# One graph kernel on Trainium2: the last 20 of 28 edge groups woven with the first 20 of 40 list groups

## The chip, the cores and the metric

The kernel runs on one core of a Trainium2 chip. The metric is device time in microseconds, the median of several executions. The core has TensorE (PE, matmuls and transposes), VectorE (DVE), ScalarE (ACT), GpSimd (POOL, which here issues all gathers and scatters) and SyncE (SP, which issues most plain DMAs). Each engine runs its own list of instructions in order and waits on semaphores for the others.

## The reference

Four graph layers over 100,000 nodes with 48 features and 50,000 edges, each followed by a residual sum and a layer norm. Cut to what matters:

```python
x = ln(x + gin(x))        # neigh = segment_sum(relu(x[src] + edge_feat), dst); (1 + eps) x + neigh
x = ln(x + appnp(x))      # 10 times: f = 0.9 * segment_sum(f[src] * w, dst) + 0.1 * x
x = ln(x + rgcn(x))       # relu MLP of 8 relations per edge, segment_sum over dst, relu
x = ln(x + edgeconv(x))   # segment_max over dst of theta(x[dst] - x[src]) + phi(x[src])
```

The kernel works on edges sorted by their target, in groups of 512 (`GE`). For edges whose source itself has incoming edges it keeps compact "lists", so that second-order terms (pairs), third-order terms and the later powers touch only list rows.

## The kernel before, in words

There are 100 edge groups (`NG`) and, for this input, 40 groups of the first list (the gather of the first pair stage is issued 160 times, four per group). `U = 4` groups make a turn. A chain of stages follows one another, each a `Block` on all five engines, closed by a barrier and by one semaphore clear after another on SP (`Scope.__exit__`, L102). The stages of interest:

- **Edge stage, tag `b_`** (`second_stage`, L1188 on; called with `FIRST = 7` turns, 28 groups). For each group, PE transposes the source rows (`columns`), applies the first weights for eight relations (`first`, three 128x512 matmuls in two passes), ScalarE applies relu (`hidden`), PE the second weights (`second`), DVE scales and scans along the edges (`weigh`, `add_up`, `highest`), PE turns the scans back into rows (`sums`), and DVE and ScalarE run three layer norms that trail by 0, 2 and 3 groups. The norm that trails by 3 groups ends in `norm4_end` (L1508, then the multiplication that writes `xob`, in the helper `scaled`, L1444). Four indirect DMAs on GpSimd (`scatter`, L1335, `after=3`) then write `xob` to the output. `part(work, i, s, k)` calls `work` for the group `k` back.
- The list of pairs is made ready meanwhile: `prepare_lines` and `run_lines` on DVE, `run_moves` on ScalarE after groups 0, 3, 4 and 7. Its last step (step 4, L1142) writes row 3 of `lists`.
- **First pair stage, `level(0, upper_rows)`**, tags `l_` in the profile (L1628 on). For each list group SP loads its numbers (`load`, L1668) and its keep row (`load_keep`), ScalarE casts the row numbers (`stage`), GpSimd gathers 4 x 128 rows of 97 floats (`fetch`, L281), DVE multiplies them by their weights (`message`, L1857 to L1864), PE transposes (`columns`), DVE scans (`add_up`, L1891), PE transposes back (`sums`), DVE takes row ends and compares places with column numbers (`run_end`, `one_hots`, L288), and PE packs the ends by 8 narrow matmuls (`pack_up`, L294), which SP stores (`put_list`).
- After it `prepare(1, ...)` and `level(1, ...)` follow, then `steps()`, where the other 72 edge groups (tag `e_`) run beside list groups of the powers, in an order written out by hand.

The order on GpSimd is what matters for the change. Before, the two stages have one kind of GpSimd work each:

```python
turns(pool, body, FIRST)      # edge stage: scatter of the group three back
drain(body, FIRST, 3)
...
part(fetch, i, s, 0, end)     # pair stage: the gather of each list group
```

Of the kernel before, what the change touches and what calls it, by code (L numbers as in the profile page):

```python
# [18 lines left out]
P, T = 128, 4  # L19
# [10 lines left out]
LINE = N // HP  # L30
EARLY = 32
FIRST = 7
WOVEN = 4
HALF = LINE // 2
ROWS = 20
# [75 lines left out]
def gnn(nc, a, out):  # L111
    ctx = ExitStack()
    with ctx:
# [89 lines left out]
        def slots(name, shape, dt=F32, n=U, scope=ctx):  # L203
            return [scope.enter_context(nc.sbuf_tensor(f"{name}{s}", shape, dt)) for s in range(n)]
# [920 lines left out]
        def run_moves(q, step):  # L1125

            (ends, firsts, places, carry), (s_places, s_chain, s_line, s_first, s_carry, s_out) = run_tiles, run_marks
            if step == 0:
                q.wait_ge(s_line, 1)
                q.dma_start(line_first[0].rearrange("(g e) -> g e", e=1), ends[1][:, 0:1]).then_inc(s_first, 16)  # L1130
            if step == 1:
                q.wait_ge(s_first, 16)
                q.dma_start(firsts[0][0:1, 0:NG], line_first[0].rearrange("(o g) -> o g", o=1)).then_inc(s_first, 16)
            if step == 2:
                q.wait_ge(s_line, 2)
                q.dma_start(line_first[1].rearrange("(o g) -> o g", o=1), firsts[1][0:1, 1:NG + 1]).then_inc(s_carry, 16)
# [13 lines left out]
        def prepare_lines(dve, k, made):  # L1150

            (now, before, after, keep, pen, kind), hot, (total, extra), (s_in, s_total, s_out, s_cnt, s_keep, s_end, s_hot) = made
            dve.wait_ge(s_total, 16)
            nc.vector.tensor_scalar(extra[:, :], total[:, :], float(GE * LU[k] - 1 - 3 * GE * LU[k]), float(GE * LU[k] * (WOVEN - 2)) if k == 2 else 0.0, ALU.add, ALU.max).then_inc(s_cnt, 1)
# [36 lines left out]
        def second_stage(scope, tag, lo, turns_n, psH, carried):  # L1191
# [18 lines left out]
            nb, kp = slots(f"{tag}nb", [F, GE], scope=scope), slots(f"{tag}kp", [XL, GE], scope=scope)  # L1210
# [62 lines left out]
            def scalar_part(act):  # L1273

                def square(k, i, s):
                    y, d, q = big[k]
                    d = rt[s][:, :, 2 * F:3 * F] if k == 2 else d
                    act.wait_ge(s_cen[k], i * U + s + 1)
                    nc.scalar.activation(q[:, :, :], d[:, :, :], ACT.Square).then_inc(s_sq[k], 1)
# [32 lines left out]
                def body(i, s, end=None):  # L1312
                    part(copy_x, i, s, 0, end)
                    part(lambda *z: square(2, *z), i, s, 0, end)
                    part(copy_d, i, s, 3, end)
# [225 lines left out]
        sc = slots("sc", [XL, GE], n=2)  # L1541

        with Scope(nc) as scope:
            first_list = preparation(0, scope)
            sync_part, scalar_part, pool_part, tensor_part, vector_part = second_stage(scope, "b_", 0, FIRST, bank[2:5], False)

            with nc.Block() as block:
                @block.sync
                def _(sp):
                    body, finish = sync_part(sp)  # L1550
                    turns(sp, body, FIRST)
                    drain(body, FIRST, 5)
                    finish()

                @block.scalar
                def _(act):
                    prepare_moves(act, 0, first_list, 3, 6)
                    run_moves(act, 0)
                    body = scalar_part(act)

                    def moving(i, s):
                        body(i, s)
                        if isinstance(i, int) and (i, s) in ((0, 0), (0, 3), (1, 0), (1, 3)):
                            run_moves(act, 1 + ((0, 0), (0, 3), (1, 0), (1, 3)).index((i, s)))

                    turns(act, moving, FIRST)
# [5 lines left out]
                def _(pool):  # L1572
                    run_places(pool)
                    body, finish = pool_part(pool, 3)
                    turns(pool, body, FIRST)
                    drain(body, FIRST, 3)
                    finish()

                @block.tensor
                def _(pe):  # L1580
                    head, tail = tensor_part(pe)

                    def body(i, s, end=None):
                        head(i, s, end)
                        tail(i, s, end)

                    turns(pe, body, FIRST)
                    drain(body, FIRST, 3)

                @block.vector  # L1590
                def _(dve):
                    parts = vector_part(dve)
                    dc = prepare_lines(dve, 0, first_list)

                    def body(i, s, end=None):
                        for work in parts:
                            work(i, s, end)
                        if isinstance(i, int) and (i, s) == (0, 2):
                            run_firsts(dve, dc)
                        if isinstance(i, int) and (i, s) == (1, 2):  # L1600
                            run_last(dve, dc)

                    turns(dve, body, FIRST)
                    drain(body, FIRST, 3)

        idxb, idx3, oi2, idxr = (sb(n, [P, NC], I32) for n in ("idxb", "idx3", "oi2", "idxr"))
        w_2 = sb("w_2", [P, NC])

        def first_rows(name, tables, clear):

# [287 lines left out]

                        drained(dve, body, 1, n)

        first_rows("pairs", level_rows[0:1], (idxb, idxr))
        level(0, upper_rows)
        prepare(1, 8, 10)
        level(1, level_rows[0])
        prepare(2, 12, 14)
# [867 lines left out]
```

## Time and profile before

| what | value |
|---|---|
| median of 3 runs | 4120.73 us (4113.66 to 4122.2) |
| the profiled execution | 4121.21 us, its span 4119.4 us |
| DVE, POOL, PE busy over the span | 69%, 63%, 60% |
| edge stage `b_`, from its first norm to its last scatter | 1358.9 to 1650.4 us |
| first pair stage, from its first load to its last store | 1669.2 to 1903.0 us |

Times in the trace count from the start of the span. A busy engine is not by itself the bound: the row to look for is the one that shows which wait of a stage ends last. The sum of the prediction is made against the profiled execution.

### The profile page before, as it was taken

The page shows a single profiled execution, that of the slowest core. Times are in us where ns is not written, and L with a number is a line of the kernel's source. Part 1 is how long each engine was busy: PE and PEld are TensorE (multiplying, and loading weights), DVE is VectorE, ACT ScalarE, POOL GpSimd, SP SyncE. Part 2 cuts the span into 40 slices and gives each one's busy share as a digit, 9 for nine tenths or more (in the row PEclk, how much of TensorE's full clock was granted, in tenths as well). Part 3 has the DMA queues.
Part 4 walks back from the last instruction along what each step waited for, and adds up shares of the span by engine and source line. Part 5 has one row for each costly group of instructions (what it writes and reads, how often), then busy time and mean ns, then how long its engine had stood idle before and what let it go on. Part 6 is the DMA issues. An engine that isn't in the chain of part 4 may idle for free. (4 is left out here: it accounts for less than half of the span.)

```text
span 4119.4 us, 57270 instructions
## 1 busy us (share of the span) xinstructions
PE 2456.7 (60%) x9282; PEld 1230.9 (30%) x9282; DVE 2823.3 (69%) x7287; ACT 1330.6 (32%) x4663; POOL 2604.9 (63%) x2529
## 2 busy tenths in 40 slices
PE   3730000277777797595644998888871009976664
PEld 2520000133333354231112554444440003333332
DVE  7989999799997787584322888887872325654333
ACT  0023333355554354131111444444431114431111
POOL 4747775377775144674754677767776766647776
PEclk9975555699999898797775999999985559985555
DMA  6947777688887443454225656656642662321111
GB/s 211 405 152 213 217 215 213 174 207 208 204 205 162 142 143 113 93 137 85 65 52 105 158 150 151 150 141 152 145 125 71 193 157 64 73 59 38 38 37 25
DMA packets 496345, 581.57 MB, mean 141 GB/s; under 512 B 218575, under 2 KB 369944, under 8 KB 491204
## 3 DMA queue, kind: packets, MB, share of 16 engines
q1 hardware_dynamic: 352858, 415.22, 32.9%
q0 software_dynamic: 87040, 90.63, 15.4%
q10 hardware_dynamic: 56306, 74.24, 5.7%
q14 instruction: 101, 0.83, 0.1%
q8 instruction: 40, 0.66, 0.1%
HBM read 276.73 MB, written 309.62 MB: 142 GB/s over the span
## 5 line engine op out<-in xcount | busy, mean ns | idle before, releaser
L505 POOL DMA_INDIRECT xdst<-in_x,dstc x400 | 459.0, 1147 | 233.5 <-issue 146.6
L281 POOL DMA_INDIRECT gb<-nodes,ib x400 | 386.7, 967 | 224.0 <-issue 126.2
L265 PE MATMUL bank<-ident,act 128*99 128x128 f32 x400 | 67.7, 294 | 645.3 <-ACT act L907 635.0
L1335 POOL DMA_INDIRECT out<-e_xob,e_ob x288 | 300.9, 1045 | 93.0 <-issue 85.6
L301 PE MATMUL bank<-chosen,rec 128*6 128x512 bf16 x1200 | 294.0, 398 | 0.6 <-ACT packed L898 0.6
L281 POOL DMA_INDIRECT cgb<-layer,ib x160 | 175.5, 1097 | 118.7 <-ACT ib L2403 72.2
L281 POOL DMA_INDIRECT ugb<-nodes,ib x160 | 166.4, 1040 | 128.8 <-ACT ib L1977 66.1
L265 PEld LDWEIGHTS bank<-ident,act 128*99 128x99 f32 x400 | 49.0, 171 | 658.0 <-issue 658.0
L294 PE MATMUL bank<-l_chosen,l_rec 128*3 128x512 f32 x480 | 242.3, 653 | 0.0
L1335 POOL DMA_INDIRECT out<-b_xob,b_ob x112 | 114.7, 1024 | 199.3 <-DVE b_xob L1444 173.4
L275 PE MATMUL bank<-ident,scan 99*128 99x99 f32 (+2 forms) x1120 | 199.5, 303 | 64.7 <-DVE scan L2170 34.1
L1384 PE MATMUL bank<-e_bxT,w 105*128 105x512 f32 x432 | 226.5, 640 | 9.3 <-ACT e_bxT L1290 8.7
L275 PEld LDWEIGHTS bank<-ident,scan 99*128 99x128 f32 (+2 forms) x1120 | 156.8, 212 | 242.7 <-issue 242.0
L1401 PE MATMUL bank<-mixer,sc 112*128 112x112 f32 x800 | 207.4, 403 | 28.1 <-issue 23.5
L1365 PE MATMUL bank<-e_hm,w 128*48 128x512 f32 x432 | 220.9, 651 | 0.0
L583 PE MATMUL bank<-hot_at,hot_no 128*125 128x400 f16 x800 | 156.0, 339 | 96.3 <-DVE hot_at L609 96.3
L281 POOL DMA_INDIRECT dgb<-layer,ib x160 | 156.2, 976 | 81.9 <-issue 47.8
L1401 PEld LDWEIGHTS bank<-mixer,sc 112*128 112x128 f32 x800 | 194.4, 327 | 37.9 <-issue 37.6
L281 POOL DMA_INDIRECT l_gp<-upper_rows,ib x160 | 160.4, 1002 | 70.4 <-issue 42.1
L2631 POOL DMA_INDIRECT out<-xo,dob x160 | 159.5, 997 | 54.3 <-issue 47.5
L281 POOL DMA_INDIRECT mhr<-rt_rows,ib x160 | 152.8, 955 | 64.6 <-issue 44.2
L265 PE MATMUL bank<-ident,l_msg 128*99 128x128 f32 (+1 forms) x280 | 59.0, 347 | 216.3 <-DVE l_msg L1864 216.0
(334 smaller groups left out, 7002.2 us busy)
## 6 DMA issues: line engine op xcount, KB each, us to landing
nodes<-wt SPq DMA_DIRECT2D x40, 1286.2 KB
lone_rows<-gb ACTq DMA_DIRECT2D x100, 294.0 KB
e_lsb<-lone_rows SPq DMA_DIRECT2D x72, 294.0 KB
rt_rows<-e_rt SPq DMA_DIRECT2D x72, 288.0 KB
parents<-zeros SPq DMA_DIRECT2D x21, 960.0 KB
upper_rows<-tb SPq DMA_DIRECT2D x100, 194.0 KB
deep_sum<-zeros SPq DMA_DIRECT2D x20, 960.0 KB
layer<-zeros SPq DMA_DIRECT2D x20, 960.0 KB
```

Of the source, the lines that this page charges most:

```text
L265: last = nc.tensor.transpose(slot(dst_ps[0:w, :], t), rows_sb[:, t, c0:c0 + w], ident[:, :])
L275: last = nc.tensor.transpose(dst_ps[:, t, 0:w], slot(cols_sb[0:w, :], t), ident[0:w, 0:w])
L281: yield nc.gpsimd.indirect_dma_start(out=dst[s][:, t, 0:width], out_offset=None, in_=table, in_offset=bass.IndirectOffsetOnAxis(ap=ib[s][: ...
L294: last = nc.tensor.matmul(ps[0:w, :], rec[:, t, :], chosen[:, t, :], start=t == 0, stop=t == T - 1)
L301: last = nc.tensor.matmul(ps[0:w, :], rec[:, k, t, :], chosen[:, t, :], start=t == 0 and k == 0, stop=t == T - 1 and k == K3 - 1)
L505: nc.gpsimd.indirect_dma_start(out=xdst[:, k * F:(k + 1) * F], out_offset=None, in_=a["x"], in_offset=bass.IndirectOffsetOnAxis(ap=dstc[:, ...
L583: last = nc.tensor.matmul(psC[h], hot_no[b][:, t, 0:HP], hot_at[b][:, t, h * HALF:(h + 1) * HALF], start=first and t == 0, stop=final and ...
L1335: nc.gpsimd.indirect_dma_start(out=out, out_offset=bass.IndirectOffsetOnAxis(ap=ob[s][:, t:t + 1], axis=0), in_=xo[s][:, t, :], in_offset= ...
L1365: last = nc.tensor.matmul(psM[0:F, :], w2[:, q, :], hm[b][q][:, :], start=q == 0, stop=q == RC - 1)
L1384: nc.tensor.matmul(psH[(s * RC + q) % HB if HB < RC else q][:, :], w1[:, q * P:(q + 1) * P], xT[s][:, :], start=True, stop=True).then_inc( ...
L1401: last = nc.tensor.matmul(psR[:, t, 0:XL], slot(sc[b], t), mixer[:, :], start=True, stop=True)
L2631: nc.gpsimd.indirect_dma_start(out=out, out_offset=bass.IndirectOffsetOnAxis(ap=ob[s][:, t:t + 1], axis=0), in_=xo[s][:, t, :], in_offset= ...
```

## The change

The two stages become one `Block`. Eight edge groups run alone (`AHEAD = 2` turns), then 20 edge groups run with one list group beside each (`BESIDE = 5` turns), then four more list groups beside the three steps in which the edge pipeline empties, then the remaining list groups in a loop as before. While woven, list group `l` has single PSUM banks (`single(i)`); the hidden layer of the edge stage has two banks (`bank[2:4]`) where it had three, for all 28 groups. The tile `nb` is now part of `kp`. The barrier, the clears and `first_rows` between the stages are gone; the two memsets and the store of a zero row stand at the head of the merged block, with four small loads. The count of turns has a floor of 7 where it had 3. The core of the diff:

```diff
-            sync_part, scalar_part, pool_part, tensor_part, vector_part = second_stage(scope, "b_", 0, FIRST, bank[2:5], False)
+            sync_part, scalar_part, pool_part, tensor_part, vector_part = second_stage(scope, "b_", 0, FIRST, bank[2:4], False)
+            alone, slots_of = AHEAD * U, BESIDE * U
...
@@ sync
+                    for g in range(alone):
+                        body(*slot_of(g))
+                    n = listed(sp)
+                    sp.wait_ge(s_prepared, 16 * (3 + R))
+                    sp.wait_ge(s_placed, 16)
+                    load(0, 0)
+                    load(0, 1)
+                    for l in range(slots_of + U):
+                        load(*slot_of(l + 2))
+                        load_keep(*slot_of(l))
+                        if l < slots_of:
+                            body(*slot_of(alone + l))
+                        else:
+                            body(*slot_of(alone + l), l - slots_of)
+                        past(store, l, 2)
+                        past(store_list, l, 4)
...
@@ scalar
+                        if l < slots_of:
+                            body(*slot_of(alone + l), between=rows_in_time)
...
+                        record(*slot_of(l))
+                        past(unpack, l, 3)
+                        stage(*slot_of(l + 2))
@@ gpsimd
-                    turns(pool, body, FIRST)
-                    drain(body, FIRST, 3)
+                    for g in range(alone):
+                        body(*slot_of(g))
+                    n = listed(pool)
+                    fetch(0, 0)
+                    fetch(0, 1)
+                    for l in range(slots_of + U):
+                        if l < slots_of:
+                            body(*slot_of(alone + l))
+                        elif l < slots_of + 3:
+                            body(*slot_of(alone + l), l - slots_of)
+                        if l + 2 < slots_of + U:
+                            fetch(*slot_of(l + 2))
+                    with pool.Fori(BESIDE + 1, n) as i:
+                        for s in range(U):
+                            fetch(i, s)
@@ tensor
+                        head(*at)
+                        past(sums, l, 1)
+                        columns(*slot_of(l))
+                        tail(*at)
+                        past(pack_up, l, 2)
@@ vector
+                    dve.wait_ge(s_kt, 16 * U)
+                    message(0, 0)
+                    for l in range(slots_of + U):
+                        head(*at)
+                        past(run_end, l, 1)
+                        middle(*at)
+                        add_up(*slot_of(l))
+                        spreads(*at)
+                        message(*slot_of(l + 1))
+                        ends(*at)
```

`body` is the edge stage's own, `load`, `stage`, `fetch`, `message`, `add_up`, `run_end`, `columns`, `sums`, `pack_up` are the functions of `level` for `k = 0`, moved here. `past(work, l, lag)` calls `work` for list group `l - lag`. In a slot `l`, GpSimd thus issues the scatter of edge group `8 + l - 3` and then the gather of list group `l + 2`.

## Rows read from the trace of the kernel before

**Rows 1.** Windows: edge steady, pairs steady, seam between; later woven stage of the powers.
```profile
core 0: us, PE busy (x) PEld busy (x) DVE busy (x) ACT busy (x) POOL busy (x), PEclk, DMA share, GB/s
1435.50:1614.50 179.00, 168.33 (x606) 92.35 (x606) 152.73 (x401) 90.58 (x228) 77.80 (x76) 0.96 0.46 144
1697.00:1880.30 183.30, 171.04 (x564) 57.00 (x561) 152.47 (x487) 58.57 (x280) 140.61 (x141) 1.00 0.59 134
1623.70:1697.00 73.30, 17.12 (x55) 9.55 (x54) 26.83 (x82) 8.97 (x44) 35.50 (x36) 0.53 0.23 56
...
2340.00:2940.00 600.00, 536.88 (x2055) 296.11 (x2054) 498.29 (x1233) 265.75 (x676) 425.09 (x408) 0.92 0.60 150
```

**Rows 2.** Groups of instructions: three of the edge stretch, one of the pairs.
```profile
L1335 POOL DMA_INDIRECT out<-b_xob,b_ob x76 | 77.8, 1024 | 101.2 <-DVE b_xob L1444 83.9 <-issue 17.4
...
L1401 PE MATMUL bank<-mixer,sc 112*128 112x112 f32 x152 | 39.8, 405 | 10.7 <-issue 10.7
...
L1303 ACT ACTIVATE b_hm<-bank,bias 128x512 f32<-128x512 f32 x57 | 34.7, 677 | 0.0
...
L281 POOL DMA_INDIRECT l_gp<-upper_rows,ib x141 | 141.6, 1005 | 43.0 <-issue 36.6 <-ACT ib L1730 5.5 <-ACT l_rec L1742 0.6
```

**Rows 3.** Timeline across the seam and to gather 24 (start us, us, engine, line).
```profile
1614.45 0.35 DVE L1451 SCALAR_TENSOR_TENSOR b_rt<-b_xa 128x192 f32<-128x192 f32 x1
...
1649.41 0.98 POOL L1335 DMA_INDIRECT out<-b_xob,b_ob  x1 [0.30 <-issue]
...
1666.24 0.25 SPq L1617 DMA_DIRECT2D nodes<-zrow  x1
...
1672.33 0.99 POOL L281 DMA_INDIRECT l_gp<-upper_rows,ib  x1 [21.94 <-ACT ib L1730]
...
1678.58 0.17 DVE L1857 TENSOR_SCALAR l_msg<-l_gp 128x12 f32<-128x12 f32 x1 [11.37 <-DMA l_gp<-upper_rows,ib]
...
1797.88 0.94 POOL L281 DMA_INDIRECT l_gp<-upper_rows,ib  x1 [0.30 <-issue]
```

**Rows 4.** Instructions of two source lines in the seam (ns min/median/max, first and last start).
```profile
L1547 POOLq DRAIN  x1: 9210/9210/9210, 1651.8 to 1651.8; - x1
...
L102 SPq EVENT_SEMAPHORE_RANGE_CLEAR  x84: 25/28/49, 1661.2 to 1668.0; - x84
```

**Rows 5.** Timeline: links from a scatter's data to the next message.
```profile
1500.82 0.36 DVE L1444 TENSOR_TENSOR b_xob<-b_bd_,b_br_ 128x192 f32<-128x192 f32 x1
...
1502.00 0.98 POOL L1335 DMA_INDIRECT out<-b_xob,b_ob  x1 [4.13 <-DVE b_xob L1444]
...
1676.14 0.94 POOL L281 DMA_INDIRECT l_gp<-upper_rows,ib  x1 [0.30 <-issue]
...
1786.07 0.94 POOL L281 DMA_INDIRECT l_gp<-upper_rows,ib  x1 [0.30 <-issue]
...
1789.71 0.20 ACT L1740 COPY l_rec<-l_gp 128x4 f32<-128x4 f32 x1 [1.27 <-DMA l_gp<-upper_rows,ib]
...
1887.70 0.17 DVE L1857 TENSOR_SCALAR l_msg<-l_gp 128x12 f32<-128x12 f32 x1 [2.48 <-DMA l_gp<-upper_rows,ib]
...
1888.84 0.35 DVE L1871 TENSOR_TENSOR l_y<-l_lt 128x192 f32<-128x192 f32 x1
```

**Rows 6.** Timeline: first relu input of the stage, and the end of its eighth group.
```profile
1359.84 0.58 ACT L1290 COPY b_bxT<-bank 96x512 f32<-96x512 f32 x1 [29.72 <-DVE line_after L1171]
...
1434.14 0.30 ACTq L1142 DMA_DIRECT2D lists<-line_ends  x1
...
1435.53 0.36 DVE L1451 SCALAR_TENSOR_TENSOR b_rt<-b_xa 128x192 f32<-128x192 f32 x1
...
1436.40 0.98 POOL L1335 DMA_INDIRECT out<-b_xob,b_ob  x1 [4.21 <-DVE b_xob L1444]
...
1440.43 0.98 POOL L1335 DMA_INDIRECT out<-b_xob,b_ob  x1 [0.30 <-issue]
```

More of the change, by code:

```diff
@@ L1209, in second_stage @@
             xT = slots(f"{tag}bxT", [RK, GE], scope=scope)
[L1210 removed]
+            kp = slots(f"{tag}kp", [XL, GE], scope=scope)
+            nb = [z[0:F, :] for z in kp]
             hm = [slots(f"{tag}hm{b}", [P, GE], n=RC, scope=scope) for b in range(2)]
@@ L1541, in gnn, with lt_, se, single @@
         sc = slots("sc", [XL, GE], n=2)
+        idxb, idx3, oi2, idxr = (sb(n, [P, NC], I32) for n in ("idxb", "idx3", "oi2", "idxr"))
+        w_2 = sb("w_2", [P, NC])
         with Scope(nc) as scope:
             first_list = preparation(0, scope)
-            sync_part, scalar_part, pool_part, tensor_part, vector_part = second_stage(scope, "b_", 0, FIRST, bank[2:5], False)
+            s_row = scope.sem("b_row")
+            s_count, s_prepared, s_placed = first_list[3][3], first_list[3][2], run_marks[5]
+            sync_part, scalar_part, pool_part, tensor_part, vector_part = second_stage(scope, "b_", 0, FIRST, bank[2:4], False)
+            assert AHEAD + BESIDE == FIRST
+            alone, slots_of = AHEAD * U, BESIDE * U
+            def lt_(name, w, n=2):
+                return slots(f"l0_{name}", [P, T, w], n=n, scope=scope)
+            def se(name, n=None):
+                if n is None:
+                    return scope.sem(f"l0_{name}")
+                return [scope.sem(f"l0_{name}{j}") for j in range(n)]
+            gp, lc = lt_("gp", PW, U), slots("l0_lc", [P, 4, T], scope=scope)
+            msg, lt, rec, y0 = lt_("msg", MW), lt_("lt", PW), lt_("rec", 3, U), lt_("y0_", F)
+            chosen = slots("l0_chosen", [P, T, GE], n=2, scope=scope)
+            packed = slots("l0_packed", [MW, GE], n=2, scope=scope)
+            base = slots("l0_base", [1, 1], I32, n=U, scope=scope)
+            lkb = slots("l0_keep", [MW, GE], scope=scope)
+            place, pf, pg = (scope.enter_context(nc.sbuf_tensor(f"l0_{n}", [P, T], F32)) for n in ("place", "pf", "pg"))
+            s_lc, s_lk = se("lc", U), se("lk", U)
+            s_g = [sem(f"l0_g{s}") for s in range(U)]
+            s_ltw, s_yw = se("ltw", 2), se("yw", 2)
+            (s_stage, s_msg, s_lcols, s_scan, s_lrows, s_cr, s_rec, s_hot, s_pack, s_packed, s_lw, s_lt, s_y0, s_pl, s_kt) = (
+                se(n) for n in ("stage", "msg", "cols", "scan", "rows", "cr", "rec", "hot", "pack", "packed", "lw", "lt", "y0", "pl", "kt"))
+            def single(i):
+                return isinstance(i, int) and i <= BESIDE
+            def columns_bank(i, s):
+                return bank[1] if single(i) else (bank[2], bank[1])[s % 2]
+            def rows_bank(i, s):
+                return wide(bank[4] if single(i) else (bank[3], bank[4])[s % 2], MW)
+            def pack_bank(i, s):
+                return (bank[0] if single(i) else (bank[5], bank[0])[s % 2])[2 * F:MW, :]
+            def slot_of(l):
+                return divmod(l, U)
+            def past(work, l, lag):
+                if l >= lag:
+                    work(*slot_of(l - lag))
+            def listed(eng):
+                eng.wait_ge(s_count, 3)
+                return turns_of(eng, 0)
@@ new lines, in _ @@
+                    body(*slot_of(alone + slots_of + U), U)
+                    with sp.Fori(BESIDE + 1, n) as i:
+                        for s in range(U):
+                            turn(i, s)
+                    for j in range(4):
+                        turn(n + j // U, j % U, j)
+                    for b in range(2):
+                        sp.wait_ge(s_lc[b], 16 * n + 16)
+                        sp.sem_inc(sp_turn, 1)
+                        sp.wait_ge(s_ltw[b], 16 * (U // 2) * n)
+                        sp.wait_ge(s_yw[b], 16 * (U // 2) * n)
+                        sp.sem_inc(sp_turn, 1)
@@ L1559, in _ @@
                     body = scalar_part(act)
[L1561 to L1566, printed above, removed]
-                    drain(body, FIRST, 3)
+                    for g in range(alone):
+                        body(*slot_of(g))
+                        if g in (0, 3, 4, 7):
+                            run_moves(act, 1 + (0, 3, 4, 7).index(g))
+                    n = listed(act)
+                    stage(0, 0)
+                    stage(0, 1)
+                    for l in range(slots_of + U):
+                        rows_in_time = lambda: past(from_rows, l, 1)
+                        if l < slots_of:
+                            body(*slot_of(alone + l), between=rows_in_time)
+                        elif l < slots_of + 3:
+                            body(*slot_of(alone + l), l - slots_of, rows_in_time)
+                        else:
+                            rows_in_time()
+                        record(*slot_of(l))
+                        past(unpack, l, 3)
+                        stage(*slot_of(l + 2))
+                    with act.Fori(BESIDE + 1, n) as i:
+                        for s in range(U):
+                            turn(i, s)
+                    for j in range(3):
+                        turn(n + j // U, j % U, j)
                     run_moves(act, 5)
@@ L1572, in _, with fetch @@
                 def _(pool):
+                    def fetch(i, s):
+                        g = i * U + s
+                        wait(pool, s_msg, g - U + 1)
+                        wait(pool, s_rec, g - U + 1)
+                        pool.wait_ge(s_stage, g + 1)
+                        pool.sem_inc(pool_turn, 1)
+                        for ins in gather(s, upper_rows, gp, PW):
+                            ins.then_inc(s_g[s], 16)
                     run_places(pool)
                     body, finish = pool_part(pool, 3)
-                    turns(pool, body, FIRST)
-                    drain(body, FIRST, 3)
+                    for g in range(alone):
+                        body(*slot_of(g))
+                    n = listed(pool)
[4 more added lines that the diff above has]
+                            body(*slot_of(alone + l))
+                        elif l < slots_of + 3:
+                            body(*slot_of(alone + l), l - slots_of)
+                        if l + 2 < slots_of + U:
+                            fetch(*slot_of(l + 2))
+                    with pool.Fori(BESIDE + 1, n) as i:
+                        for s in range(U):
+                            fetch(i, s)
                     finish()
@@ L1581, in _, with columns @@
                     head, tail = tensor_part(pe)
[L1583 to L1588, printed above, removed]
+                    def columns(i, s):
+                        g, b = i * U + s, s % 2
+                        pe.wait_ge(s_msg, g + 1)
+                        wait(pe, s_scan, g if single(i) else g - 1)
+                        pe.sem_inc(pe_turn, 1)
+                        to_columns(columns_bank(i, s), msg[b], MW).then_inc(s_lcols, 1)
@@ new lines, in pack_up @@
+                    def pack_up(i, s):
+                        g, b = i * U + s, s % 2
+                        pe.wait_ge(s_hot, g + 1)
+                        pe.wait_ge(s_rec, g + 1)
+                        wait(pe, s_packed, g if single(i) else g - 1)
+                        pe.sem_inc(pe_turn, 1)
+                        into = pack_bank(i, s)
+                        for t in range(T):
+                            last = nc.tensor.matmul(into, rec[s][:, t, :], chosen[b][:, t, :], start=t == 0, stop=t == T - 1)
+                        last.then_inc(s_pack, 1)
@@ new lines, in sums, with turn @@
+                    def sums(i, s):
+                        g, b = i * U + s, s % 2
+                        pe.wait_ge(s_scan, g + 1)
+                        wait(pe, s_cr, 2 * g if single(i) else 2 * (g - 1))
+                        pe.sem_inc(pe_turn, 1)
+                        to_rows(rows_bank(i, s), scan[b], MW).then_inc(s_lrows, 1)
+                    def turn(i, s, end=None):
+                        part(columns, i, s, 0, end)
+                        part(pack_up, i, s, 2, end)
+                        part(sums, i, s, 0, end)
@@ new lines, in _ @@
+                    for g in range(alone):
+                        head(*slot_of(g))
+                        tail(*slot_of(g))
+                    n = listed(pe)
+                    for l in range(slots_of + U):
+                        at = (*slot_of(alone + l), None if l < slots_of else l - slots_of)
+                        if l < slots_of + 3:
+                            head(*at)
+                        past(sums, l, 1)
+                        columns(*slot_of(l))
+                        if l < slots_of + 3:
+                            tail(*at)
+                        past(pack_up, l, 2)
@@ L1590, in _ @@
+                    sums(*slot_of(slots_of + U - 1))
+                    with pe.Fori(BESIDE + 1, n) as i:
+                        for s in range(U):
+                            turn(i, s)
+                    for j in range(2):
+                        turn(n + j // U, j % U, j)
                 @block.vector
                 def _(dve):
-                    parts = vector_part(dve)
+                    for z in (idxb, idxr):
+                        nc.vector.memset(z[:, :], 0)
+                    head, middle, spreads, ends = vector_part(dve)
@@ L1593, in _, with message @@
                     dc = prepare_lines(dve, 0, first_list)
[L1595 to L1598, printed above, removed]
+                    def message(i, s):
+                        g, b = i * U + s, s % 2
+                        dve.wait_ge(s_g[s], (i + 1) * 16 * T)
+                        wait(dve, s_lcols, g - 1)
+                        nc.vector.tensor_scalar(msg[b][:, :, 2 * F:MW], gp[s][:, :, 2 * F:PW].to_broadcast([P, T, 3]), 0.0, None, ALU.is_gt)
+                        nc.vector.tensor_scalar(pf[:, :], lc[s][:, 0, :], float(OFF), None, ALU.add).then_inc(s_pl, 1)
+                        dve.wait_ge(s_pl, 3 * g + 1)
+                        nc.vector.scalar_tensor_tensor(out=pg[:, :], in0=gp[s][:, :, 2 * F], scalar=0.0, in1=pf[:, :], op0=ALU.is_equal, op1=ALU.mult).then_inc(s_pl, 1)
+                        dve.wait_ge(s_pl, 3 * g + 2)
+                        nc.vector.tensor_tensor(col(idxb, g), pg[:, :], gp[s][:, :, 2 * F], ALU.add).then_inc(s_pl, 1)
+                        nc.vector.tensor_tensor(msg[b][:, :, 0:2 * F], gp[s][:, :, 0:2 * F], lc[s][:, 2, :].unsqueeze(2).to_broadcast([P, T, 2 * F]), ALU.mult).then_inc(s_msg, 1)
@@ new lines, in add_up @@
+                    def add_up(i, s):
+                        g, b = i * U + s, s % 2
+                        dve.wait_ge(s_lcols, g + 1)
+                        dve.wait_ge(s_lk[s], (i + 1) * 32)
+                        wait(dve, s_lrows, g - 1)
+                        wait(dve, s_scan, g)
+                        start = 0.0 if not begun(i, s, 1) else scan[1 - b][0:MW, GE - 1:GE]
+                        nc.vector.tensor_tensor_scan(scan[b][0:MW, :], lkb[s][:, :], columns_bank(i, s)[0:MW, :], start, ALU.mult, ALU.add).then_inc(s_scan, 1)
@@ L1599, in body, with turn @@
+                    def turn(i, s, end=None):
+                        part(message, i, s, 0, end)
+                        part(run_end, i, s, 1, end)
+                        part(add_up, i, s, 0, end)
+                    for g in range(alone):
+                        for work in (head, middle, spreads, ends):
+                            work(*slot_of(g))
+                        if g == 2:
                             run_firsts(dve, dc)
-                        if isinstance(i, int) and (i, s) == (1, 2):
+                        if g == 6:
@@ L1601, in body @@
                             run_last(dve, dc)
[L1603 to L1607, printed above, removed]
+                    n = listed(dve)
+                    dve.wait_ge(s_kt, 16 * U)
+                    message(0, 0)
+                    for l in range(slots_of + U):
+                        at = (*slot_of(alone + l), None if l < slots_of else l - slots_of)
+                        edges = l < slots_of + 3
+                        if edges:
+                            head(*at)
+                        past(run_end, l, 1)
+                        if edges:
+                            middle(*at)
+                        add_up(*slot_of(l))
+                        if edges:
+                            spreads(*at)
+                        if l + 1 < slots_of + U:
+                            message(*slot_of(l + 1))
+                        if edges:
+                            ends(*at)
@@ L1609, in first_rows @@
+                    with dve.Fori(BESIDE + 1, n) as i:
+                        for s in range(U):
+                            turn(i, s)
+                    turn(n, 0, 0)
         def first_rows(name, tables, clear):
```

87 lines of the change are left out of this document (81 added, 6 removed).

## The prediction

> **What bounds the kernel now.** I read the page first: no engine is busy for more than 69% of the span, so the stages that the change touches have to be read one by one. The windows by stage came next [rows 1]. The edge stage steadily takes 9.4 us a group (179 us for 19 groups), and PE is busy for 168.3 of the 179 us: 8.9 us a group, DVE 8.0. The pair stage takes 5.24 us a group (183.3 us for 35 groups), PE 4.9, DVE 4.4. There GpSimd is the pacemaker: each of its four issues takes 1.005 us and about 0.3 us pass before the next [rows 2]. Between the two steady stretches lie 73.3 us in which PE works for 17.1 at a clock of 0.53 [rows 1]. The timeline shows what the seam is made of [rows 3]: the edge stage would have begun a 29th group at about 1623.7 (1614.45 + 9.3). Its last scatter is issued at 1649.4, and the first gather of the next stage at 1672.3. In between, GpSimd drains for 9.2 us and SP clears 84 semaphores one by one from 1661.2 on [rows 4]. The reader is to see 48.6 us (1623.7 to 1672.3) that a merged stage could save, and then that PE needs 8.9 + 4.9 = 13.8 us for a pair of groups of which 9.4 + 5.24 = 14.6 are paid now. Weaving itself can win at most 0.8 us a pair; the seam is the prize.
>
> **What a woven slot costs.** The order on GpSimd decides. In slot `l` it scatters the edge group three back and then gathers list group `l + 2`. That scatter waits for `xob`, which DVE writes in `ends`, the last thing in its slot `l`. DVE's `message(l + 1)` stands before `ends` in the same slot, and it waits for gather `l + 1`, which GpSimd issued in slot `l - 1` behind the scatter of that slot. So one ring closes each slot, and each link has a row:
> - start of `xob` to the first scatter, 1.18 us (1500.82 to 1502.00) [rows 5];
> - four scatters to the next issue, 4 x (1.024 + 0.30) = 5.3 us [rows 2];
> - first to fourth gather, 3 x (1.005 + 0.30) = 3.9, with some jitter 4.0 us [rows 2];
> - fourth issue until its data are used: 2.44 us when nothing else moves (1676.14 to 1678.58), 3.64 in the full pair stage (1786.07 to 1789.71, an engine waiting for it) [rows 3, 5]. The pairs run at a DMA share of 0.59. A woven slot would carry 0.46 x 9.4 + 0.59 x 5.24 = 7.4 us of work per DMA engine, 0.47 of 15.7 us [rows 1]. It lies nearer to the full stage: I take 3.3;
> - `message` up to where the next DVE instruction starts, 1.14 us (1887.70 to 1888.84) [rows 5], and the two short ends ahead of `xob`, some 0.76 us by their durations: 1.9 us.
>
> Sum: 1.18 + 5.3 + 4.0 + 3.3 + 1.9 = 15.7 us a slot. The other engines fit under it: PE 13.8, DVE 8.0 + 4.4 = 12.4, GpSimd's own issues 10.5. PE then waits some 2 us a slot for the transposed message. With the shortest of each link (0.98 and 0.94 us issues, 2.44 of landing) the ring is 1.18 + 5.1 + 3.7 + 2.4 + 1.9 = 14.3 us; with 4.2 us of landing and one long issue it is 16.9.
>
> The Trainium skill (DMA: Bandwidth & Descriptors, section Anatomy of one DMA — SWDGE (gpsimd) path) gives a gather's latency as about 2.0 us fixed plus bytes over 436 GB/s. For 50 KB that is an estimate of 2.1 us, and by it the ring would be 14.5 us and the whole forecast 4117 instead of 4143. The trace disagrees for the loaded stage, 3.64 us against 2.44 [rows 5].
>
> **Entry.** DVE starts its ninth group at 1435.53. Step 4 of the list's moves leaves ScalarE at 1434.14 [rows 6], and SP now waits for its landing before it loads. GpSimd still scatters until 1440.43 + 1.29 = 1441.7, which is later than the load and the cast, so the first gather is issued at 1441.7. From first gather to first message took 6.25 us (1672.33 to 1678.58) [rows 3]: 1448.0. After `message(0)` (1.14), `head`, `middle`, the list's scan and `spreads` are some 8.6 us of DVE work (8.0 of the group, less 1.0 of ends, plus a 1.27 us scan and small waits): `message(1)` at 1457.7. Queued behind the wait of DVE are `weigh` and the scans, and PE's `sums` behind these, so the whole edge pipeline stands for about 12 us. After a pause PE's clock is at 1.2 GHz, as in the seam (0.53 of 2.4) [rows 1]; doubling `first`, `columns` and `own` of one slot costs 4.6 us, none at best, 8 at worst: I take 3.
>
> **From there to gather 24.** This is where GpSimd is alone again and both kernels go on at 5.24 us a group. After: 1457.7 + 3 + 22 rings of 15.7 (345.4) + the last links up to the next gather, 1.9 + 1.18 + 5.3 = 8.4: gather 24 at 1814.5. The three slots in which the edge pipeline empties are among the 22, since scatter and gather are still chained there. Before: 1797.9 [rows 3]. Loss: 16.6 us. Check of the before side: 20 x 9.4 + 48.6 + 125.6 (24 gathers) = 362 us, against 379 after.
>
> **Moved and added parts.** The semaphore clears of the edge stage don't vanish; they now follow the merged stage, where nothing hides them: 84 of them took about 4.8 us (1661.2 to just before 1666.24) [rows 3, 4]: +4.8. GpSimd's drain of 9.2 us is gone, as GpSimd's last gather is issued long before the stage ends. The memsets (0.8 us) and five small loads on SP (about 2 us) at the head are hidden: ScalarE waits until 1359.84 for the list's lines [rows 6]; uncovered they would cost 3. Two hidden banks instead of three make the third `first` matmul wait for a relu of 0.68 us. PE idles 10.7 / 19 = 0.56 us a group before `sums` anyway [rows 2], so I cost it at nothing, at most 0.7 x 8 = 5.6 us. The single list banks cost nothing: a slot is longer than the chain that frees them. SP gets seven list DMAs a slot beside the edge's nine; sixteen issues of under half a microsecond fit into 15.7 us, and none of the list's waits is for something of the same slot. The floor of 7 turns changes nothing with 10 turns.
>
> **Sum.** 16.6 + 4.8 = 21.4 us on the profiled execution's 4121.2: 4142.6, and the median of the runs is within 0.5 us of that execution. Break-even is a ring of 15.7 - 21.4 / 22 = 14.7 us.
>
> **Rivals.**
> - *Faster: PE sets the slot.* If the gather lands before DVE has finished `spreads`, the ring is slack and the slot is PE's 13.8 us. It decides once landing plus issue gaps fall below 13.8 - 1.9 - 1.18 = 10.7 us in all, where I count 12.6. For it: each engine fits under 13.8, and the later woven stage runs steadily [rows 1]. Against it: even the shortest row of each link gives 14.3, and in that later stage the gather is issued ahead of the scatter. It gives 22 x 1.9 = 41.8 less, and no clock loss: 4098. Chance 0.15.
> - *No change: the same ring with short landings*, 14.4 to 15.1 us. 4114 to 4129. Chance 0.22.
> - *Much slower: GpSimd's issues stretch.* An undisturbed issue of the pair stage takes 0.94 us and the mean is 1.005, so some are longer [rows 2, 5]. If all eight of a slot took 0.3 us more, the ring would be 18.1 and the time 4196. Against it: the means hold that already, and only one or two of a slot's eight can meet DVE's four comparisons. Chance 0.05, and a ring above 16.9 for another reason (PE at the half clock in many slots) 0.05. The Trainium skill (SBUF — State Buffer, section Who interferes with whom) says that descriptor writing on GpSimd is locked out while DVE runs such a comparison in a two-port mode, which speaks against weaving the two; by it alone the mean rises only in proportion to the overlap.
> - *The forecast*, a ring of 15.1 to 16.9 us: 4129 to 4170. Chance 0.53.
>
> **How the numbers follow.** 0.2% is 8 us, about what a measurement of this kernel can tell from no change. Faster 0.16, same 0.22, slower 0.62. The range reaches from 4100 (most of the PE case is left out below, about 0.1) to 4170 (0.1 above).
>
> **What the profile after would show.** If I am right: message to message 15.7 us in the woven part; DVE idle before the message, put down to the gather's DMA; GpSimd idle some 6 us a slot before the scatter, put down to `xob`; PE idle about 2 us a slot; message 1 near 1458 and gather 24 near 1814. The forecast is wrong if slots are near 13.8 us with PE never idle, or if the granted clock falls clearly below the 0.92 of the later woven stage.

## The result, and the profile after

The changed kernel takes 4213.1 us, the median of four runs (4206.43 to 4217.39), against 4118.77 for the kernel before (4113.66 to 4122.2) on the same chip. The ratio is 1.0216, 95% interval 1.0202 to 1.0230: slower, and by 94 us where the forecast was 21, outside its range. The profiled execution has a span of 4211.3 us (4119.4 before).

Nearly all of the loss is there before GpSimd is alone again. The gather of list group 24 starts at 1888.63, and at 1797.88 before [rows 3]: +90.8. The next stage's first load of the list's length is issued at 2003.55 (1906.55 before): +97.0 (5.3 of the 6.2 us that come on top are semaphore clears, below). The rest of the kernel gives 5 us back, about as much as single runs differ. So the woven slots had to be read one by one. Message to message on VectorE they take 14.8 to 15.1 us in slots 1 to 3, 18.8 in slot 4, then 20.5 in slots 5 to 19, 19.2 in slot 20 and 14.4 to 15.1 in the last three. (Slot `l` here is the time from the first instruction of `message(l)` to that of `message(l + 1)`.) The forecast was 15.7 throughout.

The windows of the kernel after, as [rows 1]: the head of the woven part (`message(0)` starts at 1451.5), then thirteen slow slots, then the last slots, then the list alone. PEclk is the granted clock of TensorE as a share of 2.4 GHz.

```profile
core 0: us, PE busy (x) PEld busy (x) DVE busy (x) ACT busy (x) POOL busy (x), PEclk, DMA share, GB/s
1452.00:1510.00 58.00, 45.51 (x159) 23.19 (x160) 47.97 (x136) 23.22 (x74) 25.45 (x26) 0.91 0.43 118
1545.40:1811.80 266.40, 192.12 (x624) 82.88 (x624) 158.20 (x456) 88.52 (x261) 103.22 (x104) 0.83 0.36 101
1811.80:1896.00 84.20, 52.57 (x158) 19.31 (x158) 42.80 (x134) 20.59 (x80) 42.94 (x42) 0.78 0.27 74
1896.00:1978.00 82.00, 74.93 (x240) 24.89 (x240) 65.37 (x210) 27.05 (x119) 58.10 (x59) 0.97 0.60 127
```

In a slow slot (266.4 / 13 = 20.5 us) no engine is near its limit: TensorE is busy for 14.8 us, VectorE 12.2, GpSimd 7.9. So engines wait for each other in a circle. The waits of twelve slow slots (1545 to 1790) say who waits for whom; the columns are the waiting engine and tile, the releaser, us in total, times, longest:

```profile
POOL out L1339 <- DVE b_xob L1448: 114.3, 11, 10.4
PEld bank L1793 <- issue: 111.1, 84, 6.0
DVE b_mw L1466 <- PE bank L1369: 94.2, 12, 7.9
PE bank L1793 <- ACT l_packed L1706: 68.6, 12, 5.9
ACT b_bxT L1292 <- PE bank L266: 67.3, 12, 5.7
```

GpSimd waits longest (for `xob`, as the forecast said), but a waiting engine at the end of a chain only repeats the delay. The row that the forecast had no place for is the fourth: TensorE, before `pack_up` (L1793), stands for 5.7 us a slot until ScalarE's `unpack` (L1706) has freed the one pack bank. Everything behind it follows: `to_columns` of the next edge group (L266) with ScalarE's `bxT`, `second` (L1369), VectorE's `weigh` (`b_mw`), at last `xob`. The forecast expected VectorE to wait for the gather's DMA; that row is missing in these slots. The page of the whole execution has the pack wait too; the last columns are the idle time of the engine just before these matmuls and what ended it. The kernel before had 0.0 there, for its 480 of them:

```profile
L1793 PE MATMUL bank<-l_chosen,l_rec 128*3 128x512 f32 x320 | 178.4, 710 | 116.4 <-ACT l_packed L1706 116.4
```

The timeline closes the circle. From one `unpack` to the next, in one slow slot (`pack_up` is L1793, `unpack` L1706, the list's comparisons L289, the roots of the layer norms L1286, `copy_rows` L1312):

```profile
1607.52 0.58 ACT L1706 COPY l_packed<-bank 3x512 f32<-3x512 f32 x1
...
1608.36 5.07 PE L1793 MATMUL bank<-l_chosen,l_rec 128*3 128x512 f32 x8 [5.69 <-ACT l_packed L1706]
...
1613.36 0.64 PE L266 MATMUL bank<-ident,b_lsb 128*96 128x128 f32 x4
...
1614.03 0.58 ACT L1292 COPY b_bxT<-bank 96x512 f32<-96x512 f32 x1 [5.62 <-PE bank L266]
...
1614.40 2.31 PE L1369 MATMUL bank<-b_hm,w 128*48 128x512 f32 x5
...
1616.75 0.68 DVE L1466 TENSOR_TENSOR b_mw<-bank,b_kp 48x512 f32<-48x512 f32 x1 [7.85 <-PE bank L1369]
...
1621.42 1.68 DVE L289 TENSOR_SCALAR l_chosen<-iota,l_place 128x512 f32<-128x512 f32 x4
...
1624.95 0.36 DVE L1434 SCALAR_TENSOR_TENSOR b_bd_<-b_bm_,b_by_ 128x192 f32<-128x192 f32 x1
...
1626.78 0.56 ACT L1286 ACTIVATE b_bs_<-b_bu_,lneps 128x4 f32<-128x4 f32 x2 [1.07 <-DVE b_bu_ L1440]
...
1627.24 0.46 ACT L1312 COPY b_rt<-bank 128x384 f32<-128x384 f32 x1
...
1628.02 0.58 ACT L1706 COPY l_packed<-bank 3x512 f32<-3x512 f32 x1
...
1628.85 1.86 PE L1793 MATMUL bank<-l_chosen,l_rec 128*3 128x512 f32 x2 [5.71 <-ACT l_packed L1706]
```

`unpack(l - 3)` frees a bank that TensorE filled one slot earlier, long before. But it stands nearly last in ScalarE's slot, behind the roots and `copy_rows` of the edge groups in flight. TensorE's `pack_up(l - 2)` stands last in its slot and ahead of the first matmul of the next one. So the pass of a slot must end before the next may begin. It has four parts: 0.84 us from `unpack` to the pack; 8.39 on TensorE, the pack's 5.07 with `to_columns` and `second`; 10.03 on VectorE from `weigh` over the scans, the list's comparisons and the norms to the roots; 1.24 on ScalarE from the roots over the copy to the next `unpack`. That makes 20.5 us from 1607.52 to 1628.02.

The ring that the forecast did describe is there too, in the slots in which the pack bank doesn't bind. Slot 1 in the timeline:

```profile
1463.79 1.02 POOL L1339 DMA_INDIRECT out<-b_xob,b_ob  x1 [12.44 <-DVE b_xob L1448]
...
1469.00 1.19 POOL L282 DMA_INDIRECT l_gp<-upper_rows,ib  x1 [0.30 <-issue]
...
1473.07 0.94 POOL L282 DMA_INDIRECT l_gp<-upper_rows,ib  x1 [0.31 <-issue]
...
1478.61 1.02 POOL L1339 DMA_INDIRECT out<-b_xob,b_ob  x1 [4.60 <-DVE b_xob L1448]
```

```profile
1475.61 0.17 DVE L1839 TENSOR_SCALAR l_msg<-l_gp 128x12 f32<-128x12 f32 x1 [1.97 <-DMA l_gp<-upper_rows,ib]
...
1477.39 0.36 DVE L1448 TENSOR_TENSOR b_xob<-b_bd_,b_br_ 128x192 f32<-128x192 f32 x1
```

The scatters take 5.21 us, the gathers 4.07 up to the fourth issue, the landing 2.54, `message` and the ends 1.78, and 1.22 us pass from the start of `xob` to the scatter: 14.82 us.

### The profile page after: what moved, and what is told of

It reads as the page before. It is cut to its first block and busy times, and to the rows that moved or that the text cites. A ratio compares the mean times of both kernels' runs of the same rounds, so it can differ in the third digit from the quotient of the medians.

```text
span 4211.3 us, 55981 instructions
## 1 busy us (share of the span) xinstructions
PE 2493.8 (59%) x9282; PEld 1229.8 (29%) x9282; DVE 2817.1 (67%) x7287; ACT 1342.1 (32%) x4663; POOL 2597.3 (62%) x2529
## 5 line engine op out<-in xcount | busy, mean ns | idle before, releaser
L266 PE MATMUL bank<-ident,act 128*99 128x128 f32 x400 | 68.0, 295 | 636.2 <-ACT act L908 632.2
L302 PE MATMUL bank<-chosen,rec 128*6 128x512 bf16 x1200 | 306.7, 410 | 0.6 <-ACT packed L899 0.6
L1793 PE MATMUL bank<-l_chosen,l_rec 128*3 128x512 f32 x320 | 178.4, 710 | 116.4 <-ACT l_packed L1706 116.4
L266 PEld LDWEIGHTS bank<-ident,act 128*99 128x99 f32 x400 | 49.7, 173 | 647.5 <-issue 647.5
L1369 PE MATMUL bank<-e_hm,w 128*48 128x512 f32 x432 | 220.7, 651 | 0.0
L1405 PE MATMUL bank<-mixer,sc 112*128 112x112 f32 x800 | 206.4, 401 | 14.4 <-issue 11.5
L266 PE MATMUL bank<-ident,cgb 128*48 128x128 f32 x160 | 24.9, 279 | 257.6 <-DMA cgb<-layer,ib 257.6
```

The costliest lines, as they stand in the source:

```text
L266: last = nc.tensor.transpose(slot(dst_ps[0:w, :], t), rows_sb[:, t, c0:c0 + w], ident[:, :])
L302: last = nc.tensor.matmul(ps[0:w, :], rec[:, k, t, :], chosen[:, t, :], start=t == 0 and k == 0, stop=t == T - 1 and k == K3 - 1)
L1369: last = nc.tensor.matmul(psM[0:F, :], w2[:, q, :], hm[b][q][:, :], start=q == 0, stop=q == RC - 1)
L1405: last = nc.tensor.matmul(psR[:, t, 0:XL], slot(sc[b], t), mixer[:, :], start=True, stop=True)
L1793: last = nc.tensor.matmul(into, rec[s][:, t, :], chosen[b][:, t, :], start=t == 0, stop=t == T - 1)
```

## The experiments

Theory A: the single pack bank, freed too late in ScalarE's queue, sets the slow slots; under it lies GpSimd's ring of 14.8 us. Theory B: GpSimd's ring is what makes the slots long, and the pack wait only fills idle time. They differ in what opening each circle alone gives. The expectations also name a Theory C: the two hidden banks, or TensorE's order as a whole, make the slot. Each experiment has a profile and was timed in three rounds against the kernel before. The first four shared 19 runs of it (median 4125.82), the last three 9 (4124.99).

**The bank is freed earlier.** ScalarE runs `unpack(l - 3)` in front of the edge group's hidden copies, right after `from_rows`:

```diff
-                        rows_in_time = lambda: past(from_rows, l, 1)
+                        rows_in_time = lambda: (past(from_rows, l, 1), past(unpack, l, 3))
...
                         record(*slot_of(l))
-                        past(unpack, l, 3)
```

> One edit to the changed kernel: on ScalarE, while woven, the unpacking of list group l-3 stands with the row copies of group l-1 near the head of slot l, where it stood last in the slot. Theory A (the single pack bank sets the slot: PE's pack of group l-2 waits for an unpack that ScalarE does only after the layer norms of the same slot, 5.7 us of waiting and a late next group): the 17 slots of 20.5 us fall to about 15.0, the length of slots 1 to 3, and the time to about 4213 - 17 x 5.5 = 4120 us. Theory B (the ring of GpSimd's scatter, gather and the next message sets the slot, as predicted, only longer than predicted): no change, 4213. Theory C (two instead of three hidden banks, or the hand-written order of PE as a whole, makes the slot): no change, 4213.

Measured: 4124.03 us, ratio 0.9995 (0.9983 to 1.0007). The slots are 14.8 us all along (14.2 to 15.3, and two of 16.3 and 16.5); gather 24 starts at 1797.75, 90.9 us earlier than in the changed kernel. The pack wait is gone, and the waits (1540 to 1700) now show the ring, with the wait for the gather that the forecast had named:

```profile
POOL out L1339 <- DVE b_xob L1448: 41.7, 9, 5.1
...
DVE l_msg L1838 <- DMA l_gp<-upper_rows,ib: 21.3, 10, 3.7
```

So one copy of 0.58 us, moved within its queue, is worth all that the change lost, and what remains is neither faster nor slower than the kernel before. Theory C expected no change and falls with it. No run gave the pack its second bank back, so this shows the price of the place in the queue, and not what a second bank would give.

**The gather is issued earlier.** GpSimd fetches list group `l + 2` before it scatters in slot `l`; the bank stays as it was:

```diff
                     for l in range(slots_of + U):
+                        if l + 2 < slots_of + U:
+                            fetch(*slot_of(l + 2))
                         if l < slots_of:
...
-                        if l + 2 < slots_of + U:
-                            fetch(*slot_of(l + 2))
```

> One edit to the changed kernel: in each woven slot GpSimd gathers list group l+2 before it scatters the edge group three back. Theory A (pack bank): the 20.5 us slots stay, only the few slots of 15 us at either end may shorten by 1 us; 4205 to 4213 us. Theory B (GpSimd's ring): every woven slot falls to PE's 13.8 us, 4213 - 17 x 6.7 - 6 x 1.2 = 4092 us.

Measured: 4213.16 us, ratio 1.0209 (1.0192 to 1.0226), the time of the changed kernel. The slots before the pack bank binds fall to 12.6 to 13.1 us, the others stay at 20.47. Theory B falls: GpSimd's ring costs nothing while the slower circle stands.

**Both together.** The two edits above.

> Both edits: unpack early on ScalarE and gather ahead of scatter on GpSimd. Theory A says that two rings lie one under the other, 20.5 us and 15.0 us, and that with both open PE's 13.8 us show: about 25 us less than with the early unpack alone, 4095 us, faster than the kernel before. If the second ring is not GpSimd's, the time is that of the early unpack alone, about 4120 us.

Measured: 4080.46 us (4066.83 to 4083.83), ratio 0.9895 (0.9878 to 0.9911). This is 1.05% under the kernel before, and under the changed kernel too. The slots are 13.2 us, and the window 1520 to 1700 shows the limit:

```profile
1520.00:1700.00 180.00, 179.74 (x655) 85.57 (x655) 166.36 (x471) 90.91 (x269) 111.78 (x110) 1.00 0.57 155
```

TensorE is busy for 179.74 of 180 us at the full clock. The three slots in which the edge pipeline empties take 9.5 to 11.8 us, where they took 14.6 to 16.3 with the bank freed early. From `message(1)` to `message(24)` the profiles have 297.2 us here and 343.0 there, 45.8 less. The full slots were expected at 13.8 and are 13.2, and the emptying ones were not expected to be shorter; together they make most of the 15 us by which the kernel came out below its expectation. (The profile is of the fastest of the four runs, 4066.83 us, so its parts are compared here and not its total.)

**The remaining ring opened from the other side.** With `unpack` early and GpSimd in its old order, VectorE does `ends(l)` before `message(l + 1)`, so `xob` no longer waits for a gather:

```diff
+                        if edges:
+                            ends(*at)
                         if l + 1 < slots_of + U:
                             message(*slot_of(l + 1))
-                        if edges:
-                            ends(*at)
```

> Unpack early as before, GpSimd in the order of the changed kernel (scatter, then gather), and on VectorE the ends of slot l ahead of message l+1. If the remaining ring is scatter, gather, landing, message, ends, this opens it from the other side as well as the earlier gather did: slots of 13.2 to 13.5 us and 4080 to 4095 us. If GpSimd's queue itself is what holds a slot at 14.8 us (scatter and gather issues plus their waits), it stays near 4124. A message later in the slot may make TensorE's columns of the next slot wait: then 14 us a slot and some 4105.

Measured: 4092.71 us, ratio 0.9932 (0.9911 to 0.9954). The slots are 13.2 and 13.5 to 13.8 us, mostly in turn. The window 1560 to 1700:

```profile
1560.00:1700.00 140.00, 139.11 (x503) 64.64 (x502) 127.89 (x368) 67.67 (x212) 88.73 (x84) 1.00 0.55 153
```

GpSimd issues what it issued before, in the same order, and TensorE is busy for 139.11 of 140 us. So it was the link from landing to `xob` that made the ring, not GpSimd's amount of work. It stays 12 us behind the earlier gather. Part of that is 0.3 us a slot: from `message(1)` to `message(24)` it takes 302.6 us against 297.2. The rest was not traced.

**Fewer woven slots.** The changed kernel with twenty edge groups alone and eight woven:

```diff
-AHEAD, BESIDE = 2, 5
+AHEAD, BESIDE = 5, 2
```

> The changed kernel with twenty edge groups alone and eight woven instead of eight and twenty. Theory A (each woven slot from the fifth on pays for the single pack bank): twelve slots of 20.5 us become twelve pairs of 9.3 + 5.24 = 14.5 us, 12 x 5.9 = 71 us less than the changed kernel, 4142 us. Theory B (the loss sits in the entry and the end of the woven part, the slots are worth no more than 15 us each): 12 x 0.5 = 6 us less, 4207.

Measured: 4139.8 us, ratio 1.0046 (1.0025 to 1.0068). The loss is one per slot and not one for the entry: twelve slots fewer gave 73 us, 6.1 each. Its trace has five such slots left (three of 20.6 to 20.8 us, one of 19.1 and one of 19.2 at the ends) where the changed kernel has seventeen.

**Fewer woven slots in the best version.** The same line changed in the kernel with both edits.

> Unpack early and gather first together (13.2 us a slot, TensorE busy throughout), but only eight groups woven. If weaving itself still wins in each slot, twelve slots of 13.2 us become 9.3 + 5.24 = 14.5 us: 12 x 1.3 = 16 us more than with twenty woven, 4096. If the gain over the kernel before comes from the missing seam alone, no difference: 4080.

Measured: 4088.12 us, ratio 0.9922 (0.9900 to 0.9945), 8 us over the version that weaves twenty. It lies between the two expectations: weaving wins 0.6 us a pair here and not 1.3. Edge groups alone take 9.0 us in this kernel, where the expectation had 9.3, which leaves 9.0 + 5.24 - 13.23 = 1.0 us a pair. The traces agree with the 1.0: from the first relu input of the edge stage to the next stage's first load of the list's length the best version takes 503.9 us with twenty woven and 515.4 with eight, 0.96 us a pair; the 0.4 us to the medians' 0.64 is within what four runs of each can tell. Twenty pairs at 0.64 to 0.96 us make 13 to 19 of the 45 us by which the best version beats the kernel before. The rest is put down to the missing seam and to the edge turns written out; no run separates these two.

**Two hidden banks.** The kernel before, with `bank[2:4]` in place of `bank[2:5]`:

```diff
-"b_", 0, FIRST, bank[2:5], False)
+"b_", 0, FIRST, bank[2:4], False)
```

> The kernel before with two hidden PSUM banks instead of three in its 28 edge groups, nothing woven. The prediction costs this at nothing, because PE idles 0.56 us a group before the sums anyway, and at most 0.7 us a group: 4119 us, at most 4119 + 28 x 0.7 = 4138. Theory C needs several us a group: 28 x 5 = 140 us more.

Measured: 4120.35 us, ratio 0.9985 (0.9972 to 0.9998). The third bank bought nothing in the kernel before. In the woven kernel two banks did not stand in the way either: with both edits TensorE is busy for 179.74 of 180 us.

## Why the prediction was wrong

**The step that failed** is "The single list banks cost nothing: a slot is longer than the chain that frees them". I compared durations: pack and unpack together last 4.2 us (3.60 and 0.58 in the version with the bank freed early), a slot 15.7. What counts is where the two stand in their queues. `unpack(l - 3)` comes at the end of ScalarE's slot and `pack_up(l - 2)` at the end of TensorE's, so the bank binds the end of one slot's pass to the start of the next. This costs 5.5 to 5.7 us a slot, seventeen slots long, and gather 24 came at 1888.63 instead of 1814.5. Moving `unpack` alone took it away, to 1797.75. The part was only looked at for its size, and the queues were not followed for it as they were for GpSimd.

**What held, by its own steps.**
- *The ring.* Every link was there, and it set the slots once the bank was out of the way: 14.8 us, or 14.95 on average with its two longer slots (1461.2 to 1790.0 for 22), whose cause was not looked for. I had 15.7. The term that was too large is the landing, 2.5 us in nearly every slot of the version with the bank freed early (last gather at 1622.05, its data used at 1624.55; three slots have 3.0) where I took 3.3, nearer to the full pair stage's 3.64 [rows 5]. The DMA share in those slots was 0.48, as estimated (0.47). With the ends first it was 0.55, near the pair stage's 0.59, and the gathers that VectorE waited for still landed in 2.4 to 2.7 us; so the share alone doesn't say how long a gather takes to land. The Trainium skill (DMA: Bandwidth & Descriptors, section Anatomy of one DMA — SWDGE (gpsimd) path) would have given about 2.1 us as its estimate, nearer than my choice; the trace shows 0.4 more.
- *The entry, in its total only, and that by luck.* `message(1)` was forecast at 1457.7 + 3 and came at 1460.8. The first gather came as forecast (1441.58 for 1441.7). But `message(0)` came at 1451.50 and not at 1448.0: its data needed 6.1 us from the fourth issue, for which the forecast's 6.25 from the first one leaves 2.4. SP had stood until 1437.25 for the list's landing and then issued the loads of the next edge groups and list groups in a row, and the DMA engines were busy for 0.94 of 1442.0 to 1451.5. TensorE stood for the same loads. From `message(0)` to `message(1)` passed 9.3 us and not 12.7, at a granted clock of 1.00: the 3 us that I had put down to a slow clock were not there. The two misses, 3.5 and 3.4 us, cancel.

```profile
1442.00:1451.50 9.50, 5.05 (x12) 1.56 (x12) 0.00 (x0) 0.58 (x1) 7.21 (x8) 0.71 0.94 249
1451.50:1460.80 9.30, 8.04 (x34) 4.98 (x35) 8.93 (x23) 3.85 (x9) 0.00 (x0) 1.00 0.07 22
...
1443.90 1.06 PE L266 MATMUL bank<-ident,b_lsb 128*96 128x128 f32 x4 [11.28 <-DMA b_lsb<-lone_rows]
...
1451.50 0.18 DVE L1839 TENSOR_SCALAR l_msg<-l_gp 128x12 f32<-128x12 f32 x1 [15.89 <-DMA l_gp<-upper_rows,ib]
```

- *The formula from there.* With the measured ring, 1460.8 + 22 x 14.95 + 8.4 gives 1798.1 for gather 24; the kernel with the bank freed early has it at 1797.75, and the kernel before at 1797.88 [rows 3]. As 14.95 was read from that same kernel, this tests only the count of rings and the last links (7.8 us there, 8.4 in the forecast). That kernel is the forecast's own rival "the same ring with short landings", and its 4124 us lie in that rival's 4114 to 4129.
- *Clears.* From the last `unpack` to the next load 10.8 us went by (1992.74 to 2003.55) against 5.5 before (1901.07 to 1906.55): +5.3 for the moved semaphore clears (111 in one block where 27 stood), forecast 4.8.
- *Hidden banks.* Costed at nothing, and nothing by the run with two of them in the kernel before.
- *TensorE as the limit.* The rival's 13.8 us became 13.2. The edge stage's 8.9 us a group were read at a clock of 0.96 [rows 1]; at 1.00, the clock of the best version, they would be about 8.5, and the pair 13.4 (an estimate from these two rows). The other 0.2 us were not traced.

**The rivals missed it too.** "A ring above 16.9 for another reason" had 0.05, with TensorE at the half clock in mind. The clock was in it as a follower: 0.83 over the slow slots, where TensorE paused 5.7 us a slot, and the pack that came right behind the pause took 5.07 us where it took 3.60 in the version with the bank freed early. The rival of stretched GpSimd issues named something real but small. In that version the first of the four gathers took 1.19 to 1.20 us for the 18 of the 24 woven list groups for which it met VectorE's comparisons, and 0.94 to 0.99 for the 6 for which it didn't: 0.2 us a slot, where the rival's price stood for 2.4.

That the order on the queues is what the bank's price hangs on is shown, by moving one instruction. The lower clock's share can be read from the two timelines: behind the pack, the groups of matmuls of a slow slot take what they take in the version with the bank freed early (`to_columns` 0.64 us in both, `second` 2.31 in both), so it is the pack's 5.07 - 3.60 = 1.5 of the 20.5 us, and the circle would be about 19.0 us at full clock (an estimate).

## What to carry to other kernels

When two pipelines are woven, check every buffer that loses its second copy for its place and not for its size: write down in which position of whose queue it is freed, in which position it is taken again, and what both engines must finish between the two. If that runs through a slot's whole pass, as here from TensorE over VectorE to ScalarE, the slots no longer overlap. Free a shared bank early in its engine's slot, ahead of what waits for results of the same slot, and issue a gather ahead of a scatter that does. Where several circles lie over each other, opening the shorter one shows nothing in the time, so judge an edit by the slots in which the longer one doesn't bind.

## What the runs showed of the hardware

The granted clock of TensorE was lower where it paused: 1.00 over 180 us where it was busy for 179.74 (both edits, 1520 to 1700), 0.98 where it was busy for 189.58 of 210 (bank freed early, 1540 to 1750), 0.83 where it was busy for 192.12 of 266.4 (the changed kernel's slow slots). Within a slow slot it was 0.50, which is 1.2 GHz, from 1608.3 to 1610.0, right behind the pause, and 1.00 again from 1611.5 on. The last gather of four landed in 2.5 us at a DMA share of 0.48, as fast as the 2.44 us in the seam [rows 3], where little else moved; in the changed kernel's entry, at a share of 0.94, it took 6.1 us. The first gather issue of a list group took 1.19 to 1.20 us on GpSimd where VectorE compared places at the same time, and 0.94 to 0.99 where it didn't (bank freed early). Edge groups alone took 9.0 us each with their turns written out (1435 to 1520 in the best version with eight woven), where the hardware loop of the kernel before takes 9.4 [rows 1]. The loop has intervals of 10.2 to 10.9 us among its groups here and there; their cause was not looked for.
